# Decoder block on one core: self-attention and cross-attention groups in alternation, side work in other slots

## What is computed

```
x = x + attn(layernorm(x))            # 16 heads of 32, causal, with q/k/v/o weights and biases
x = x + xattn(layernorm(x), ctx, ctx) # 16 heads, causal, no weights: keys and values are ctx itself
n = layernorm(x)
x = x + relu(n @ W_up.T) @ W_down.T + sum(softmax(top2(n @ W_gate.T))) * (n @ W_expert)
```

## Time and profile before

| | |
|---|---|
| median of 3 runs | 803.59 us (801.75 to 805.96) |
| the profiled execution, its own time | 806.62 us |
| its span (first to last instruction) | 804.8 us |
| TensorE busy / weight loads | 713.9 us (89%) / 535.3 us (67%) |
| VectorE, ScalarE, GpSimd busy | 504.2, 516.0, 256.3 us |
| mean granted TensorE clock | 0.966 of full |

### The profile page before, as it was taken

The page is one execution under the profiler, slowest core; times in us unless marked ns, Lnnn a source line. Parts: engine busy times, 40 slices in busy tenths (PEclk is TensorE's granted clock), DMA queues, the critical chain, the costliest instruction groups (busy, mean ns, idle before and its releaser), DMA issues.

```text
span 804.8 us, 14482 instructions
## 1 busy us (share of the span) xinstructions
PE 713.9 (89%) x4480; PEld 535.3 (67%) x4480; DVE 504.2 (63%) x1726; ACT 516.0 (64%) x1450; POOL 256.3 (32%) x390
## 2 busy tenths in 40 slices
PE   4997998979989899897779887799987999889998
PEld 3775676757766677675557554577765777667786
DVE  5566556656556565755666667766787667764532
ACT  6577676657766577756866886677667776775010
POOL 3644443324444333634640573210031112000100
PEclk9997899999999999998989898999999999999999
DMA  9542333335433354234754695233444343410001
GB/s 324 129 124 66 105 80 70 69 76 154 115 70 79 92 156 107 61 72 128 214 144 105 189 236 134 60 92 92 134 96 133 91 132 73 132 40 1 27 27 52
DMA packets 45995, 86.16 MB, mean 107 GB/s; under 512 B 8416, under 2 KB 8416, under 8 KB 45920
## 3 DMA queue, kind: packets, MB, share of 16 engines
q1 hardware_dynamic: 45920, 85.25, 40.5%
HBM read 27.55 MB, written 7.34 MB: 43 GB/s over the span
## 4 chain that ended last, share of the span: by engine, by line
PE 66%; DVE 13%; issue 8%; POOL 6%; ACT 5%; DMA 2%; SPq 1%; DVEq 0%; POOLq 0%; ACTq 0%
PE t L382 13%; PE m L412 11%; PE m L413 11%; PE m L414 11%; PE pv L406 10%; PE s L370 7%; DVE probs L558 4%; POOL probs L872 3%; DVE stats L585 2%; PE m L425 1%; ACT probs L770 1%; DVE prob L568 1%; DMA stack<-stage 1%; POOL w_lo L912 1%; DVE f_stats L592 1%
## 5 line engine op out<-in xcount | busy, mean ns | idle before, releaser
L770 ACT ACTIVATE probs<-probs,negmax 128x128 f32<-128x128 f32 (+3 forms) x512 | 285.9, 559 | 132.4 <-DVE negmax L558 126.1
L558 DVE CUSTOM_DVE_ANT_0 probs<-s,mask 128x128 f32<-128x128 f32 (+3 forms) x512 | 247.1, 485 | 172.1 <-PE s L370 169.0
L370 PE MATMUL s<-stack 96*128 96x128 f32 (+3 forms) x512 | 205.6, 402 | 51.0 <-DVE negmax L558 48.1
L382 PE MATMUL t<-ident,probs 128*128 128x128 f32 x1280 | 230.8, 281 | 10.4 <-POOL probs L872 7.0
L382 PEld LDWEIGHTS t<-ident,probs 128*128 128x128 f32 x1280 | 164.6, 144 | 62.1 <-POOL probs L872 12.0
L872 POOL TENSOR_SCALAR probs<-probs,rsum 128x128 f32<-128x128 f32 (+3 forms) x256 | 133.1, 540 | 214.0 <-DVE rsum L572 209.4
L779 ACT ACTIVATE prob<-t 128x512 f32<-128x512 f32 (+1 forms) x256 | 136.0, 531 | 82.8 <-PE t L382 82.6
L370 PEld LDWEIGHTS s<-stack 96*128 96x128 f32 x512 | 99.2, 194 | 83.7 <-DVE negmax L558 47.9
L568 DVE COPY prob<-t 128x256 f32<-128x256 f32 (+1 forms) x256 | 91.0, 356 | 20.8 <-PE t L382 20.5
L770 ACT ACTIVATION_READ_ACCUMULATOR probs<-probs,negmax 128x1 f32 x512 | 96.5, 189 | 0.0
L406 PE MATMUL pv<-prob,V 128*32 128x512 f32 (+3 forms) x1024 | 83.9, 472 | 0.0
(11 more groups left out here) (126 smaller groups left out, 897.2 us busy)
## 6 DMA issues: line engine op xcount, KB each, us to landing
stack<-stage SPq DMA_DIRECT2D x384, 128.0 KB, 2.3
xt<-in_x SPq DMA_DIRECT2D x16, 256.0 KB, 4.2
xres<-in_x SPq DMA_DIRECT2D x4, 1024.0 KB, 5.9
kraw<-in_ctxT SPq DMA_DIRECT2D x16, 256.0 KB, 2.9
V<-in_ctx SPq DMA_DIRECT2D x4, 1024.0 KB, 5.9
x<-xres SPq DMA_DIRECT2D x3, 1024.0 KB, 4.6
res<-x SPq DMA_DIRECT2D x8, 256.0 KB, 6.0
out<-res SPq DMA_DIRECT2D x2, 1024.0 KB, 4.4
```

The costliest lines, as they stand in the source:

```text
L370: nc.tensor.matmul(score_tile(P, i), stack[0:RS, P % 2, h, 0, chunk(qb)], stack[0:RS, P % 2, h, 1, 0:N], start=True, stop=True).then_inc(s ...
L382: mm = nc.tensor.transpose(dst[:, chunk(qb - kb)], probs[:, (2 * P + h) % 3, OFF[qb] + PART * kb:OFF[qb] + PART * kb + PART], ident[:, :])
L558: nc.vector.tensor_tensor_reduce(probs[:, (2 * P + h) % 3, OFF[qb]:OFF[qb + 1]], score_tile(P, i), mask[:, T - N:T], -SCALE, BIG, ALU.add, ...
L770: nc.scalar.activation(tile, tile, ACT.Exp, bias=negmax[:, P % 2, h, qb:qb + 1], scale=-1.0, accum_out=total).then_inc(p_exp, 1)
```

## The change

**Order of the groups.** A string gives the order: 14 self groups, then cross, self, cross, self, cross, cross, then 12 cross. Groups keep their place numbers G in time; `RANK[G]` is the number within its kind. So the last two self groups stand at G = 15 and 17 instead of 14 and 15, and cross batch 0 at G = 14, 16, 18, 19 instead of 16 to 19. Everything from step 40 on has the same groups as before. The fills now: 24 V; 25 O; 26 Q+O; 27 K+O; 28 O; 29 none; 30 Q; 31 K; 32 to 36 none; 37 O+O; 38 O+O; 39 to 41 none.

**Side work.** The statistics of j = 1 to 3 stand two in each of two steps (slots 0 and 1 of steps 8j-9 and 8j-8), those of j = 4 in steps 21 and 22; two of the norms of j = 1 to 3 move to the next step, those of j = 4 from step 27 to step 24. The first L transpose of a batch goes into bank `pv` in slot 4, the others to slots 5, 6 and 8 (before: 5, 6, 7 and 8). DVE empties Q and K one slot later.

**Loads and FFN weights.** The cross values are loaded a group at a time (256 KB into `cv`) instead of a batch at a time (1 MB into `V[1]`). `V[1]` now holds the raw expert and down weights, and the splits on POOL stand in steps 38 to 43 in the order expert, up, down.

```diff
+ORDER = "s" * 14 + "cscscc" + "c" * 12
+IS_SELF = [k == "s" for k in ORDER]
+RANK = [ORDER[:G].count(ORDER[G]) for G in range(NG)]
+SELF_AT = [G for G in range(NG) if IS_SELF[G]]
+CROSS_AT = [G for G in range(NG) if not IS_SELF[G]]
+SELF_END = 2 * SELF_AT[-1] + 3
...
+def own(G):
+    return 0 <= G < NG and IS_SELF[G]
+def other(G):
+    return 0 <= G < NG and not IS_SELF[G]
+def own_rank(P):
+    return 2 * RANK[P // 2] + P % 2
...
-    return PAIRS * (j - 1) + (2 if j == B + 2 else 0)
+    return PAIRS * (j - 1) + {B: -2, B + 2: 2}.get(j, 0)
+def stats_slots(j):
+    z = PAIRS * stats_step(j)
+    return [z - 8, z - 7, z, z + 1] if j <= B else [z + 1, z + 2, z + 3, z + 4]
 def norm_slots(j):
     z = PAIRS * PAIRS * (j - 1) + PAIRS * (2 if j < B else 3)
-    return [z + 4, z + 5, z + 8, z + 9] if j == B + 2 else [z, z + 1, z + 4, z + 5]
+    if j == B:
+        return [PAIRS * PAIRS * (B - 1) + i for i in (2, 3, 5, 6)]
+    return [z + 4, z + 5, z + 8, z + 9] if j == B + 2 else [z, z + 1, z + 8, z + 9] if j < B else [z, z + 1, z + 4, z + 5]
...
-    for G in range(NGS):
-        put(("Q", G), 2 * G - 4, 4 if G and G % KC == 0 else 0, 4)
-        put(("K", G), 2 * G - 3, 0, 4)
+    for n, G in enumerate(SELF_AT):
+        put(("Q", n), 2 * G - 4, 4 if n and n % KC == 0 else 0, 4)
+        put(("K", n), 2 * G - 3, 0, 4)
     for b in range(B):
         for t in range(NT):
             if b:
                 put(("V", b, t), PAIRS * b - 3 + t, 4, 4)
-                put(("L", b, t), PAIRS * b - 5, 5 + t, 1)
+                if t:
+                    put(("L", b, t), PAIRS * b - 5, 4 + t + t // 3, 1)
             else:
                 put(("V", b, t), t - 2, 4, 4)
             if b == B - 1:
-                put(("O", b, t), NPS + 1 + t // 2, 4 * (t % 2), 4)
+                put(("O", b, t), SELF_END + t // 2, 4 * (t % 2), 4)
...
+    for b in range(1, B):
+        z, key = PAIRS * (PAIRS * b - 5) + 4, ("L", b, 0)
+        bank_of[key] = 2
+        running.setdefault(z, []).append((key, 0))
+        ended.setdefault(z + 1, []).append(key)
...
-        f_raw = {UP: f_xln, EXPERT: res2, DOWN: f_xln}
+        f_raw = {UP: f_xln, EXPERT: V[1], DOWN: V[1]}
...
-            return m_bank[BANK_OF[key]]
+            return [*m_bank, pv_bank][BANK_OF[key]]
...
+            def load_values(G):
+                n = RANK[G]
+                if n >= 2:
+                    sp.wait_ge(pv_done, NT * (CROSS_AT[n - 2] + 1))
+                sp.dma_start(cv[:, n % 2, :, :], ctx_v[n // KC][:, :, chunk(n % KC)]).then_inc(v_loaded[n % 2], 16)
...
+                if s % 2 == 1 and other((s + 1) // 2):
+                    load_values((s + 1) // 2)
+                if s == SELF_END:
+                    sp.wait_ge(pv_done, NT * (SELF_AT[-1] + 1))
+                    load_weight("expert", EXPERT)
+                if s == SELF_END + 2:
                     sp.wait_ge(o_mm, NT * B)
                     load_weight("upT", UP)
-                    load_weight("expert", EXPERT)
-                if s == NPS + 5:
+                    sp.wait_ge(x2_stored[2], 16)
+                    load_x(res2, x2[2])
+                if s == SELF_END + 3:
                     sp.wait_ge(f_lo_done, KC)
                     load_weight("downT", DOWN)
-                if s == NPS + 6:
-                    sp.wait_ge(f_lo_done, 2 * KC)
-                    sp.wait_ge(x2_stored[2], 16)
-                    load_x(res2, x2[2])
...
+            def left(G):
+                if IS_SELF[G]:
+                    pe.wait_ge(cx_lo_done, RANK[G] + 1)
+                else:
+                    pe.wait_ge(c_mul, RANK[G] + 1)
...
+                    if G in L_PV:
+                        pe.wait_ge(lnt_lo, KC * L_PV[G] + 1)
+                    if G > 0:
+                        left(G - 1)
...
+                if BANK_OF[key] == 2:
+                    left(KC * key[1] - 4)
...
-                        dve.wait_ge(f_lo_done, 3 * KC)
+                        dve.wait_ge(f_lo_done, 2 * KC)
...
+                    for key in ENDED.get(z - 1, ()):
+                        if key[0] in ("Q", "K"):
+                            empty(key)
                     for key in ENDED.get(z, ()):
-                        if key[0] not in ("V", "FG"):
+                        if key[0] not in ("V", "FG", "Q", "K"):
...
-                        if s == stats_step(j) and 1 <= i <= NT:
-                            ln_stats(j, i - 1)
+                        if z in stats_slots(j):
+                            ln_stats(j, stats_slots(j).index(z))
...
-                for n, slot in enumerate((UP, EXPERT, DOWN)):
+                for n, slot in enumerate((EXPERT, UP, DOWN)):
                     for c in range(KC):
-                        if s == NPS + 4 + ((0, 0, 0, 1), (1, 1, 2, 2), (3, 3, 3, 4))[n][c]:
+                        if s == SELF_END + 1 + ((0, 1, 1, 1), (2, 2, 3, 3), (4, 4, 5, 5))[n][c]:
```

More of the change, by code:

```diff
@@ L65 @@
 RING = 6
+L_PV = {KC * b - 3: b for b in range(1, B)}
 NS, NTB = 2, 3
 FEED = (PAIRS * 42 + 4, PAIRS * 51 + 4, PAIRS * 60, PAIRS * 67 + 4)
+def own(G):
[4 more added lines that the diff above has]
+    return 2 * RANK[P // 2] + P % 2
 def feed_start(f):
@@ L253, in emptied @@
             kind, n, m = key if len(key) == 3 else (*key, 0)
-            return {"L": (lnt_lo, KC * n + m + 1), "Q": (q_lo, n + 1), "K": (k_lo, n + 1), "V": (v_out, NT * n + m + 1),
+            return {"L": (lnt_lo, KC * n + m + 1), "Q": (q_lo, SELF_AT[n] + 1 if kind == "Q" else 0), "K": (k_lo, n + 1), "V": (v_out, NT * n + m + 1),
                     "O": (o_out, NT * n + m + 1), "FL": (fl_lo, KC * n + m + 1),
@@ L280, in load_stack @@
                 sp.wait_ge(q_lo, G + 1)
[L281 to L284, removed]
+                sp.wait_ge(k_lo if IS_SELF[G] else ck_lo, RANK[G] + 1)
                 for h in range(2):
@@ L644, in empty @@
                     w, hi, lo = (WQ, QH, QL) if kind == "Q" else (WK, KH, KL)
-                    dve.wait_ge(q_hi if kind == "Q" else k_hi, n + 1)
-                    nc.vector.scalar_tensor_tensor(out=stage[:, n % 2, lo, :], in0=src[:, :],
-                                                   scalar=bias[:, w, n % KC:n % KC + 1], in1=f32(stage[:, n % 2, hi, :]),
+                    G = SELF_AT[n]
+                    if kind == "Q":
+                        dve.wait_ge(q_hi, G + 1)
+                    else:
+                        dve.wait_ge(k_hi, n + 1)
+                    nc.vector.scalar_tensor_tensor(out=stage[:, G % 2, lo, :], in0=src[:, :],
+                                                   scalar=bias[:, w, n % KC:n % KC + 1], in1=f32(stage[:, G % 2, hi, :]),
                                                    op0=ALU.add, op1=ALU.subtract)\
@@ L806, in empty @@
                     w, hi = (WQ, QH) if kind == "Q" else (WK, KH)
-                    act.wait_ge(q_mm if kind == "Q" else k_mm, n + 1)
-                    need(act, stack_in[1][1], 48 * (n - 1))
-                    nc.scalar.activation(stage[:, n % 2, hi, :], src, ACT.Identity, bias=bias[:, w, n % KC:n % KC + 1])\
+                    G = SELF_AT[n]
+                    if kind == "Q":
+                        act.wait_ge(q_mm, G + 1)
+                    else:
+                        act.wait_ge(k_mm, n + 1)
+                    need(act, stack_in[1][1], 48 * (G - 1))
+                    nc.scalar.activation(stage[:, G % 2, hi, :], src, ACT.Identity, bias=bias[:, w, n % KC:n % KC + 1])\
                         .then_inc(q_hi if kind == "Q" else k_hi, 1)
@@ L918, in f_split @@
                     pool.wait_ge(f_loaded[slot], 16)
-                    pool.wait_ge({UP: v_mm, EXPERT: q_mm, DOWN: k_mm}[slot], NGS)
+                    if slot == EXPERT:
+                        pool.wait_ge(q_mm, SELF_AT[-1] + 1)
+                    else:
+                        pool.wait_ge(v_mm if slot == UP else k_mm, NGS)
                 nc.gpsimd.tensor_copy(w_hi[:, slot, c, :], f_raw[slot][:, c, :]).then_inc(f_hi_done, 1)
@@ L930, in _ @@
                                     pattern=[[-1, PART]], channel_multiplier=1).then_inc(made, 1)
-            own = mask[:, T - PART:T]
-            nc.gpsimd.affine_select(out=own, in_=own, compare_op=ALU.is_ge, fill=MASKED, base=0,
+            square = mask[:, T - PART:T]
+            nc.gpsimd.affine_select(out=square, in_=square, compare_op=ALU.is_ge, fill=MASKED, base=0,
                                     pattern=[[-1, PART]], channel_multiplier=1).then_inc(made, 1)
```

125 lines of the change are left out of this document (62 added, 63 removed).

## The result

The changed kernel takes 775.34 us, the median of 4 runs (773.27 to 777.97), beside 804.78 (801.75 to 807.67) for the kernel before on the same chip. The ratio is 0.9609, with a 95% interval of 0.9565 to 0.9653. By that ratio 31.5 us are gone (the medians lie 29.4 apart), where 16.2 were forecast. The direction was right and the size about half; 775.34 lies at the lower end of the range from 775 to 800. The profiled execution has a span of 774.6 us and a mean granted clock of 0.969 (before 0.966); the other three runs of the changed kernel have 0.978, 0.967 and 0.980.

A forecast was written before the change was run, and what follows sets the result against it. TensorE bounds the kernel; only its idle time and lower-clock loss can be won. Terms -5.2, -2.0, -1.3, -3.6, -1.0, -5.1 and +2.0 sum to -16.2: 806.62 profiled gives 790.4, or 787 against the median; range 775 to 800.

The forecast's parts named there:

- K and Q emptied a slot later: VectorE's 32.7 us of waiting for ACT mostly lies beside a full TensorE, so moving these emptyings gives -1.0 us.
- The clock: Step behind a statistics stall: lower clock costs 1.7 us at most, seen behind one of two stalls; 1.2 taken.
- denser: Rival, chance 0.20: stalls and most of the lower clock go, light steps take 15.02 a pair; 777, range 770 to 780.
- A rule weighed: Lower clock follows gaps, not a fixed load; the skill's rule (throttled by default) would lose 6.4 us, ending near 794.
- L: Steps such as 19 and 20: first transpose's 1.61 us wait goes; 1.2 us a batch, three times, -3.6; bounds 0, -9.
- Statistics and norms: Batches 1 to 3: spread statistics remove stalls in steps 8 and 16, -5.2; norms partly moved a step on, -1.3.
- Step 24: Its four statistics and Q's fill and emptying leave, four norms come in; -2.0 us, bounds -0.5 and -4.
- Alternation: Steps 27 to 40, with -0.4 in step 25: mixed self and cross groups and moved fills give -5.1; bounds -12, +2.
- The new wait: Step 41: f_norm needs two up splits GpSimd does behind the power; VectorE waits 3 to 4 us, net +2.0.
- keep their length: Rival, chance 0.17: light self pairs wait for GpSimd's scaling regardless, alternation gives +3; 795, range 793 to 799.6.
- The slower case: Rival, chance 0.08: lower clock in steps 28 to 36; below a mean of 0.73 slower, at 0.70 810.

The follow-up runs named there:

- the splits first: Changed kernel with the two up splits of step 41 moved ahead of f_scale in GpSimd's program: 771.97 us, ratio 0.9565.
- context later: Kernel before with VectorE's low part of the context one slot later, Q and K emptied where they were: 797.37 us, ratio 0.9878.

## Why the prediction was half right

**The step that failed** is *K and Q emptied a slot later*: "mostly lies beside a full TensorE; a full pair has only 0.43 us idle (21.27 less 20.84) ... I take -1.0 for all." It measured 18 us alone and 13.5 as the last of the edits; alone, 11.8 us of it were at full clock. The wrong reading is older, in the opening: "The reader should look for windows in which width exceeds TensorE's busy time." That difference counts too little. VectorE in the second half of step 14, in the kernel before (start, length, what, idle time ahead of it):

```profile
206.91 0.29 DVE L558 CUSTOM_DVE_ANT_0 probs<-s,mask 128x128 f32<-128x128 f32 x1
...
208.77 0.75 DVE L646 SCALAR_TENSOR_TENSOR stage<-m,bias,stage 128x512 fp32r<-128x512 f32 x1 [1.57 <-ACT stage L809]
209.44 0.74 DVE L631 SCALAR_TENSOR_TENSOR cx<-pv,bias,cx 128x512 fp32r<-128x512 f32 x1
210.09 0.41 DVE L558 CUSTOM_DVE_ANT_0 probs<-s,mask 128x256 f32<-128x256 f32 x1
...
210.44 0.17 DVE L572 RECIPROCAL rsum<-rowsum 128x4 f32<-128x4 f32 x1
```

The same place in the changed kernel:

```profile
189.09 0.29 DVE L610 CUSTOM_DVE_ANT_0 probs<-s,mask 128x128 f32<-128x128 f32 x1
...
190.37 0.75 DVE L684 SCALAR_TENSOR_TENSOR cx<-pv,bias,cx 128x512 fp32r<-128x512 f32 x1 [0.99 <-ACT cx L852]
191.04 0.41 DVE L610 CUSTOM_DVE_ANT_0 probs<-s,mask 128x256 f32<-128x256 f32 x1
191.38 0.17 DVE L624 RECIPROCAL rsum<-rowsum 128x4 f32<-128x4 f32 x1
191.47 0.72 DVE L703 SCALAR_TENSOR_TENSOR stage<-m,bias,stage 128x512 fp32r<-128x512 f32 x1
```

From the maximum of 128 columns to the next, 256, it is 3.18 us before (206.91 to 210.09) and 1.95 after: the emptied bank stands behind both now, and its high part has long been there. TensorE before, around the score matmul that waits for that maximum:

```profile
209.76 0.38 PE L382 MATMUL t<-ident,probs 128*128 128x128 f32 x2
...
210.57 0.50 PE L370 MATMUL s<-stack 96*128 96x512 f32 x1 [0.43 <-DVE negmax L558]
...
212.93 0.66 PE L382 MATMUL t<-ident,probs 128*128 128x128 f32 x4 [0.23 <-POOL probs L872]
```

And after:

```profile
191.94 0.38 PE L425 MATMUL t<-ident,probs 128*128 128x128 f32 x2
192.08 0.48 PE L410 MATMUL s<-stack 96*128 96x512 f32 x1
```

Without a wait the score matmul starts 0.14 us behind the transposes' start, with it 0.81: the loss is 0.67 us, of which the bracket shows 0.43, since the transposes' modelled end (209.76 + 0.38) lies 0.24 past the point at which the next matmul could have started. The reciprocal is late in the same way; through GpSimd it holds up the first transposes of the odd step, the last row of before, 0.45 us for a bracket of 0.23. The Trainium skill (Perfetto Trace Analysis, "Identifying the Most-Contended Engine") says that TensorE's matmul busy share is no good measure of headroom, because pipelined matmuls look smaller there. Here they look longer than their share of the time (a fill's matmuls are 0.40 us long and start 0.23 us apart), but the trace agrees that this sum misleads: 20.84 busy fell to 20.58 with not a matmul less, while the weight loads' sum stayed at 15.97 and 15.93.

**The clock** is the second step that failed. The prediction counted one step at the lower level, 17, and 1.2 us for it. Six had it in steps -1 to 28, with up to 12 us lost, and all six lost it. So its *denser* rival, by which "the stalls go and take most of the lower clock with them", was right there and wrong behind step 28. How much of the 31.5 us is clock and how much idle time was not measured apart. Nor does the lower level simply follow a gap, as *A rule weighed* has it: step 16 is 14.19 both in the kernel before and with L alone, and step 17 behind it has 0.84 in the one and 1.00 in the other.

**L** was mis-sized: -3.6 forecast, 10.4 alone. The prediction took 1.2 of each 4.24 us idle in steps 19 and 20. That pair, at full clock, gave 1.6, but steps 3 and 4 3.9 and steps 11 and 12 3.1: there the clock of steps 4 and 12 rose too, which the sum did not have, as it did in step 17 (1.1). Where its wait would stand was forecast rightly, before the second L and for the stage's low part, with 2.9 us idle left in steps 19 and 20 (26.24 less 23.34):

```profile
245.08 0.66 PE L479 MATMUL m<-ident,xt 128*128 128x128 f32 x4 [1.40 <-DVE stage L703]
```

And "K is now emptied a slot later, behind O" was right as a cost: steps 11 and 19 take 12.06 and 12.08 in the changed kernel with the early emptying, 12.87 and 12.88 with the late one.

**Statistics and norms** were mis-sized too: -5.2 and -1.3, where 9.4 were measured. The mechanism stood as forecast: no idle time before the last score matmul of steps 8 and 16. The clock of step 17 is 1.00 instead of 0.84, but it is so with L alone or the late emptying alone as well, so it is no proof of this term. The 2.02 of each stall came out at 2.00 (14.20 to 12.20, without the late emptying). The statistics of batch 1 in step 0, 1.6 us, had been left out of the sum. The norms took 0.5 us off step 18 alone, as forecast (12.69 to 12.21); that it has no idle time left in the changed kernel (11.51 of 11.51 busy) is the late emptying's doing. **Step 24**, -2.0 forecast, gave 3.0 (14.20 to 11.21), 1.7 of it in the old order, in which Q's fill stays.

**Alternation** was forecast at -5.1 and gives nothing. Two of its parts were well read: steps 33 and 34 below 18 us (16.38) and 37 and 38 near 22 (22.80), and steps 29 and 30 took 18.50 for 18.4 forecast, 31 7.68 for 8.5, 39 and 40 14.62 for 16.8. But its -5.3 in steps 27 and 28 measured -2.9 and did not hang on the order (21.68 in the old one, 21.54 in the new): 1.3 came in step 27 (12.35 to 11.10), which the norms leave, and 1.6 in step 28, whose clock rose from 0.86 to 1.00 and rises with the late emptying alone too. Taken without that item, the prediction's own list comes to +0.2, near what the chip says; in part that is luck, since its items for steps 35 and 36 (0) and 39 and 40 (-1.4) missed by 2.2 each in opposite directions. Steps 35 and 36, put at 0, cost 2.2 (20.05 at a clock of 0.82, before 17.84 at 0.81). With a clock of 0.91 they take 18.78, in the kernel with the splits first, and in the old order at full clock 15.99, in the kernel with context later (last section), so at least 0.9 us is the exchange of self and cross pairs and not the clock.

**The new wait** was as forecast: 3 to 4 us of VectorE (4.26), +2.0 for TensorE, measured 2.45 in steps 41 and 42 (25.46 to 27.91). Taken away, it gave 3.0 in steps 40 to 42; the intervals of the two kernels' ratios overlap. In the changed kernel:

```profile
465.21 1.04 POOL L949 TENSOR_TENSOR f_rstd<-f_veps,neg_half 128x4 f32<-128x4 f32 x1
...
468.81 1.27 POOL L990 TENSOR_TENSOR w_lo<-f_xln,w_hi 128x512 fp32r<-128x512 f32 x1
470.19 0.72 DVE L671 TENSOR_SCALAR f_xln<-xt,f_mv,f_rstd 128x512 f32<-128x512 f32 x1 [4.26 <-POOL w_lo L990]
471.78 0.53 PE L458 MATMUL pv<-prob,cv 128*32 128x128 f32 x8 [2.29 <-DVE prob L620]
```

**The rivals.** The denser case, 777, came nearest in its time, and for half of its reason: the lower clock went from steps -1 to 28, but the light steps with self pairs did not come down to 15.02 a pair, and the lower clock stayed in them. The light steps did not all keep their length, 9 us or more each: 33 and 34 average 8.2, but 35 and 36 average 10.0. The slower case did not come: steps 28 to 36 have a mean clock of 0.88 (before 0.89), not below 0.8, although step 33 alone has 0.66. The rule weighed there would have taken the 6.4 us of steps 33 and 34 back; they took 16.38 at 0.84. The clock of 0.74 in steps 41 and 42 is not the wait's doing, for it is 0.76 with the wait gone.

## What to carry to other kernels

Where TensorE is the bound, cost a wait on another engine by when the next matmul starts, and compare two steps of equal work start to start; window less busy time showed 0.43 us where 1.15 were to be had, over most of self-attention. On an in-order queue, whatever frees a bank that the bound engine needs next goes ahead of whatever waits for a third engine, and a slot's delay for that other work costs nothing so long as no one is due to read it. When several edits touch the same late instruction, expect their gains to overlap (38 us apart, 28.6 together), and take from the term of a reordering whatever would move in the old order too. Read the granted clock step by step and price every step that has the lower level: a mean of 0.966 before and 0.969 after hid six such steps that went and others that came.

## What the runs showed of the hardware

The clock in light steps differs between executions of the same instructions. Steps 35 and 36 in the kernel with L alone, then in the one with context later:

```profile
429.88:447.73 17.85, 15.97 (x99) 9.68 (x97) 12.94 (x48) 12.78 (x38) 8.69 (x9) 0.81 0.83 222
```

```profile
429.76:445.75 15.99, 13.18 (x98) 8.73 (x97) 12.98 (x48) 12.76 (x38) 8.72 (x9) 1.00 0.88 246
```

The kernel before has 17.84 at 0.81 there. Step 60, whose code none of these edits touches, took 11.07 us in the profiled execution of before at clock 1.00 and 12.71 in that with context later at 0.87. So some 2 us of difference in one such place, in one profiled execution of each kernel, is no evidence for an edit, and the lower level is not fixed by the code of the step alone; what sets it here stays open. Runs of one kernel differ in it as a whole: the four of the changed kernel take 777.97, 776.63, 774.05 and 773.27 us at mean clocks of 0.967, 0.969, 0.978 and 0.980.
